# Graph attention stage of a GNN: keys computed and scattered before the queries, destination rows earlier, first loads of the edge stage in another form

## The reference

```python
Q = (x @ Wq).reshape(N, NUM_HEADS, HEAD_DIM)
K = (x @ Wk).reshape(N, NUM_HEADS, HEAD_DIM)
Q_src = Q[src]
K_tgt = K[tgt]
score = (Q_src * K_tgt).sum(axis=-1) * scale + edge_attr @ We
m = jax.ops.segment_max(score, tgt, num_segments=N)
ex = jnp.exp(score - m[tgt])
...
out = agg.reshape(N, HIDDEN) @ Wo + bo
```

## Time and profile before

| | us |
|---|---|
| median of 3 runs | 2367.73 |
| lowest and highest | 2366.19, 2367.78 |
| the profiled execution | 2364.44 |
| its span | 2362.7 |
| PE busy in the span | 1813.0 |
| DVE busy | 1230.3 |
| POOL busy | 1175.3 |
| ACT busy | 921.1 |

### The profile page before, as it was taken

One profiled execution on the slowest core, in us unless ns is written; L12 is line 12 of the kernel. 1 busy time (PEld: TensorE's weight loads), 2 busy tenths in 40 slices (PEclk: granted clock), 3 DMA queues, 4 the chain that ended last, 5 costly groups with the idle time before them and its releaser, 6 DMA issues. The chain is left out here.

```text
span 2362.7 us, 39722 instructions
## 1 busy us (share of the span) xinstructions
PE 1813.0 (77%) x12108; PEld 1537.0 (65%) x12109; DVE 1230.3 (52%) x2534; ACT 921.1 (39%) x1975; POOL 1175.3 (50%) x1175
## 2 busy tenths in 40 slices
PE   5627988887863889599950888788869449999996
PEld 4425766666653666499950776667747449999996
DVE  6527977777757521311135877777746752222221
ACT  4325765555531343344325222222224233333332
POOL 1575777777722200244425777777760014444443
PEclk9858988777776898699975999999979569999998
DMA  4397655555562110377767766666650477776775
GB/s 121 100 188 171 171 158 152 155 157 154 149 144 69 45 43 22 99 202 202 198 159 197 245 222 222 223 217 228 221 169 12 123 228 194 192 200 186 198 200 154
DMA packets 224073, 383.40 MB, mean 162 GB/s; under 512 B 38181, under 2 KB 167748, under 8 KB 223764
## 3 DMA queue, kind: packets, MB, share of 16 engines
q1 hardware_dynamic: 158988, 243.83, 33.8%
q0 software_dynamic: 64160, 136.38, 22.8%
q10 hardware_dynamic: 840, 2.16, 0.3%
HBM read 287.62 MB, written 98.35 MB: 163 GB/s over the span
## 5 line engine op out<-in xcount | busy, mean ns | idle before, releaser
L785 POOL DMA_INDIRECT qr<-q_rows,src_t x405 | 392.8, 970 | 139.4 <-issue 120.3
L1918 POOL DMA_INDIRECT fr<-f_rows,src_i x381 | 360.3, 946 | 155.5 <-issue 112.4
L1938 PE MATMUL psP<-f_part,onehot 125*128 125x256 bf16 x2925 | 358.0, 286 | 82.5 <-DVE onehot L1964 82.3
L1938 PEld LDWEIGHTS psP<-f_part,onehot 125*128 125x128 bf16 x2925 | 297.3, 103 | 136.6 <-DVE onehot L1964 90.8
L867 PE MATMUL psK<-kp,oh_k 126*128 x1680 | 286.8, 327 | 86.4 <-DVE qr L935 51.7
L867 PEld LDWEIGHTS psK<-kp,oh_k 126*128 126x128 bf16 x1680 | 189.9, 113 | 179.4 <-issue 101.7
L1976 DVE SCALAR_TENSOR_TENSOR psA<-psA,same,fr 128x256 f32<-128x256 f32 x420 | 206.4, 491 | 92.9 <-DMA fr<-f_rows,src_i 61.6
L2048 ACT ACTIVATE acc<-psA 128x1280 f32<-128x1280 f32 x84 | 103.9, 1237 | 327.3 <-DVEq L1979 320.7
L1668 ACT ACTIVATE m1hT<-m1psH,m1par 128x128 f32<-128x128 f32 x448 | 127.7, 368 | 254.0 <-PE m1psH L1688 254.0
L1688 PEld LDWEIGHTS m1psH<-m1xT,m1w 128*128 128x128 f32 x1792 | 211.0, 194 | 2.8
L1688 PE MATMUL m1psH<-m1xT,m1w 128*128 128x128 f32 x1792 | 211.2, 277 | 0.0
(11 more groups left out here) (478 smaller groups left out, 2716.6 us busy)
## 6 DMA issues: line engine op xcount, KB each, us to landing
m1w<-in_L_ffn_W_dram SPq DMA_DIRECT2D x56, 1024.0 KB, 5.9
run_rows<-acc SPq DMA_DIRECT2D x84, 640.0 KB, 3.5
m0w<-in_L_ffn_Wd_dram SPq DMA_DIRECT2D x32, 1024.0 KB, 5.5
loc<-locals_ SPq DMA_DIRECT2D x85, 157.5 KB
ea<-in_edge_attr_dram SPq DMA_DIRECT2D x84, 140.0 KB
w_all<-in_L_ffn_W_dram SPq DMA_DIRECT2D x8, 1024.0 KB
m1b<-in_L_ffn_b_dram SPq DMA_DIRECT2D x56, 128.0 KB, 2.9
qr<-q_rows,src_t POOLq DMA_INDIRECT x420
```

The lines of the kernel that those rows point to most:

```text
L785: nc.gpsimd.indirect_dma_start(out=qr[:, n % GQ, u, :], out_offset=None, in_=q_rows, in_offset=bass.IndirectOffsetOnAxis(ap=src_t[:, n, u: ...
L1918: nc.gpsimd.indirect_dma_start(out=fr[:, n % GI, u, :], out_offset=None, in_=f_rows, in_offset=bass.IndirectOffsetOnAxis(ap=src_i[:, n * G ...
L1938: last = nc.tensor.matmul(psP[:, k % 2, 0:D], onehot[:, k % 2, t, :], f_part[:, c, t, :], start=(t == 0 and c == 0), stop=(t == T - 1 and ...
```

## The change

The first stage makes the keys first and the queries last. The work on the destinations moves ahead of the statistics of groups 1 to 4. `pos_i` and the scatters no longer come after queries and gathers. ACT takes four small copies from DVE. In the edge stage, the first loads of `loc` don't wait, the keys are loaded in 5 parts (19, 15, 15, 15, 14 blocks), PE turns the edge attributes of the next group after the key expansion, and its first and last turn are written out of the loop.

```diff
-AHEAD = 3
+AHEAD = 1
...
-                store_q(0)
-                store_q(1)
                 sp.wait_ge(s_local, 2)
...
-                for i in range(2, NG):
-                    store_q(i)
+                store_q(0)
                 sp.wait_ge(s_localst, 48)
                 sp.dma_start(base_i[:], bases).then_inc(s_base, 16)
+                for i in range(1, NG):
+                    store_q(i)
...
-                pool.wait_ge(s_srck, 1)
-                pool.wait_ge(s_qst, 32 * NG)
...
-                for g in range(AHEAD - 1):
-                    gather(g)
                 pool.wait_ge(s_pos, 1)
...
-                gather(AHEAD - 1)
+                pool.wait_ge(s_srck, 1)
+                pool.wait_ge(s_qst, 32 * NG)
+                for g in range(AHEAD):
+                    gather(g)
                 pool.wait_ge(s_kst, 16 * T)
...
-                for i in range(2):
+                for i in range(NG):
                     apply_norm(i)
                     fetch_normed(i)
+                    if i == 0:
+                        first_part(0)
+                    if i == 2:
+                        first_part(1)
+                        middle_part(0)
+                        first_part(2)
+                first_part(3)
+                middle_part(1)
+                first_part(4)
                 for i in range(NG):
                     if i + 2 < NG:
-                        apply_norm(i + 2)
+                        middle_part(i + 2)
                     fetch_queries(i)
...
-            K_GROUPS = (0, 1, 2, 3)
+            K_GROUPS = (0, 1, 2, 3, 4)
...
-                load_locals(0, 0)
                 sp.wait_ge(s_eaz, 2)
                 for g in range(1, GI):
+                    load_locals(0, g - 1, reused=False)
                     load_ea(0, g, True)
                     load_k(sp, g)
-                    load_locals(0, g)
+                load_k(sp, GI)
+                load_locals(0, GI - 1)
...
+                turn_attributes(0, 0)
+                groups(0, first_turn=True)
+                with pe.Fori(1, EITER - 1) as i:
+                    groups(i)
+                groups(EITER - 1, last_turn=True)
```

More of the change, by code:

```diff
@@ L486, in key @@
                 def key(t):
+                    pe.wait_ge(s_t0, t // G + 1)
                     pe.wait_ge(s_k0e, t + 1)
@@ L506, in _, with rows @@
                 last.then_inc(s_par_turned, 1)
+                def rows(a, b):
+                    for t in range(a, b):
+                        dst_row(t)
                 turn_normed(0)
-                turn_normed(1)
[L510 to L520, removed]
@@ L521, in _ @@
-                pe.wait_ge(s_srcf, 1)
-                pe.wait_ge(s_par_kept, 1)
[L523 to L531, removed]
+                pe.wait_ge(s_w0, 32)
@@ new lines, in _ @@
+                for t in range(G):
+                    key(t)
+                pe.wait_ge(s_sel, 1)
+                pe.wait_ge(s_num, 2)
+                rows(0, 4)
+                turn_normed(1)
+                rows(4, 6)
+                key(5)
+                rows(6, 8)
+                turn_normed(2)
+                for n in range(3):
+                    key(6 + n)
+                    rows(8 + 2 * n, 10 + 2 * n)
+                key(9)
+                rows(14, 15)
+                for t in range(10, 13):
+                    key(t)
@@ L637, in _ @@
                 v.sem_inc(s_sel, 1)
[L638 to L642, removed]
+                deviations(1, 3)
+                v.wait_ge(s_const, 10)
+                ends(range(3 * G))
+                second_part(0)
+                deviations(3, NG)
+                third_part(0)
+                ends(range(3 * G, T))
+                nc.vector.scalar_tensor_tensor(end_f[:], part_n[:], float(J), end_f[:], ALU.mult, ALU.add).then_inc(s_end, 1)
+                degrees()
+                second_part(1)
+                places()
+                third_part(1)
                 v.wait_ge(s_src, 32)
                 nc.vector.tensor_copy(src_gf[:], src_g[:]).then_inc(s_srcf, 1)
+                second_part(2)
                 v.wait_ge(s_rankd, 16)
@@ L653, in _ @@
                                         ALU.subtract).then_inc(s_local, 1)
-                v.wait_ge(s_const, 10)
-                ends(range(T - 2 * G))
+                third_part(2)
+                second_part(3)
+                third_part(3)
                 v.wait_ge(s_srcT, 1)
[L657 to L668, removed]
+                nc.vector.tensor_copy(src_t[0:ET, 0:NK], psT[0:ET, 0, 0:J].rearrange("p (u k) -> p k u", u=G)).then_inc(s_srck, 1)
+                second_part(4)
+                third_part(4)
         score = sb(top, "score", [E, H, J])
@@ L844, in _ @@
                 pe.wait_ge(s_webd, 32)
-                with pe.Fori(0, EITER) as i:
-                    for g in range(GI):
[L847 to L881, removed]
-                            last = nc.tensor.matmul(psC[0:P, 0:T], oh_lo[:, g, u, :], oh_hi[:, g, u, :], start=False, stop=False,
-                                                    skip_group_check=True)
-                        last.then_inc(s_ohu, 1)
@@ new lines, in edge_scores @@
+                def edge_scores(i, g):
+                    pe.wait_ge(s_eae, i * GI + g + 1 + GI)
+                    pe.wait_ge(s_esk, i * GI + previous_use(g, 2, GI) + 1 + GI)
+                    for n in range(3):
+                        w = min(128, G * ED - n * 128)
+                        last = nc.tensor.matmul(psS[:, g % 2, n * 2 * H:n * 2 * H + w // ED * H],
+                                                eaT[0:w, g, n * E:(n + 1) * E], we2[0:w, 0:w // ED * H],
+                                                start=True, stop=True)
+                    last.then_inc(s_es, 1)
@@ new lines, in count_sources, with groups @@
+                def count_sources(i, g):
+                    pe.wait_ge(s_oh, i * GI + g + 1)
+                    for u in range(G):
+                        last = nc.tensor.matmul(psC[0:P, 0:T], oh_lo[:, g, u, :], oh_hi[:, g, u, :], start=False, stop=False,
+                                                skip_group_check=True)
+                    last.then_inc(s_ohu, 1)
+                def groups(i, first_turn=False, last_turn=False):
+                    first = named_bases(i, 0)
+                    for g in range(GI):
+                        expand(i, g, first, first_turn)
+                        if g + 1 < GI:
+                            first = named_bases(i, g + 1)
+                            turn_attributes(i, g + 1)
+                        elif not last_turn:
+                            turn_attributes(i + 1, 0)
+                        edge_scores(i, g)
+                        count_sources(i, g)
```

77 lines of the change are left out of this document (60 added, 17 removed).

## The result

| | before | after |
|---|---|---|
| median of 6 runs, us | 2367.76 | 2375.32 |
| lowest and highest | 2366.19, 2368.97 | 2373.80, 2379.24 |
| the profiled execution | 2364.44 | 2373.80 |
| first scatter, start | 87.94 | 79.03 |
| last scatter, start | 125.61 | 118.14 |

The changed kernel is slower by 7.6 us, 0.3 %: the ratio is 1.0036, with an interval of 1.0023 to 1.0049. The forecast was 2362.0, a gain. So the prediction had the wrong direction, and the time lies 6.3 us above its range.

A forecast was written before the change was run, and what follows sets the result against it. POOL's stream of gathers was taken to bound the edge stage: 123.2 + 420 x 1.274 + 1.3 = 659.6 against 665.28, 5.7 us less. Against the median 2367.73 this gave 2362.0, range 2354.5 to 2369.

The forecast's parts named there:

- What bounds the kernel: Edge stage: POOL's stream of gathers sets its end, and PE, DVE and ACT follow it.
- First scatter, 82.1: First stage: POOL's first scatter starts at 82.1 us, 5.8 earlier than 87.94.
- Last query copied, 117.0: First stage: last key leaves PE at 92.4, then 25 queries take 22 us plus 2.5 of pauses, to 117.0.
- queries at half clock: Rival, first stage: PE's clock at 0.50 makes each query 1.46 us, POOL starts at 137.9, total 2375.5; chance 0.08.
- This gives 122.0. The stores now run beside the scatters: End of first stage: query stores land 5.0 us after the last copy, plus 1.2 unhidden; first gather at 123.2.
- Ten more gathers and the stall: Edge stage: ten more gathers cost 12.7 us; the first turn's stall falls from 16.0 to 1.0 to 1.5.
- Keys in 5 parts and loads without waits, worth nothing: Edge stage's first loads: given no gain; PE may begin group 3 up to 6 us earlier, DVE still waits for `loc`.
- Pitch, 1.274 us: Edge stage: time per gather on POOL without the first turn's stall, 1.274 us, applied to 420 gathers.
- rival E: Rival from the experiments: the edge stage's edits cost 3 to 5 us at 979 ns a gather; no chance given.
- A microsecond at POOL's last gather is one of the total: After the edge stage: later stages are the same code behind the same barrier, so changes pass one to one.

The follow-up runs named there:

- e2: Changed first stage with the edge stage of the kernel before, against the kernel before: 2757.82 and 2741.52 us, ratios 1.0060 and 1.0040.
- e8: The changed kernel unaltered, run again on another chip, against the kernel before: 2762.61 us, ratio 1.0046.
- e4: Against the changed kernel, the eleventh and later scatters wait until the queries are stored: 2762.03 us.
- e7: Against the changed kernel, the eighteenth and later scatters wait until the queries are stored: 2762.11 us.
- e1: The kernel before with the edge stage of the changed one, against the kernel before: 2751.04, 2738.74, 2738.95 us, ratios 1.0005, 1.0054, 1.0028.

## Why the prediction was wrong, point by point

**What bounds the kernel: right.** In the result's executions POOL's stream of gathers still sets the end of the edge stage. Its last gather moved by +5.8 us and the profiled execution by +9.4.

**First scatter, 82.1: 3.1 us too late.** It came at 79.03. The last rows of counts and their copies ended at 69.8 instead of 72.9. The wait that I had put on key 17 is there, 3.31 us:

```profile
73.53 2.04 PE L483 MATMUL psQ<-w_qk,n_rows 128*125 128x256 f32 x4 [2.92 <-ACT k_f L443]
76.27 0.18 DVE L620 COPY tot<-psP 125x25 f32<-125x25 f32 x1 [3.31 <-PE psP L556]
```

**Last query copied, 117.0: right within 1.6.** The last key left PE at 93.2 (forecast 92.4) and the queries ran at PE's full rate:

```profile
103.50 6.74 PE L483 MATMUL psQ<-w_qk,n_rows 128*125 128x256 f32 x30 [0.18 <-ACT x L433]
```

These 30 records are 7.5 products at 0.90 us each, and the granted clock is 1.00 in the windows from 90 to 115, 2.4 GHz. So the rival "queries at half clock", which gave 2375.5, the time that came, did not happen. Only its total fits: it has the first gather at 137.9, which came at 132.14, and its mechanism is refuted. The match is luck, and it takes this row to see it.

**The step that failed: "This gives 122.0. The stores now run beside the scatters", with 1.2 us "of a bound from 0 to 3".** I had taken the 5.0 us between last copy and landing from a stretch in which nothing else was transferred, and added a bound for company. That made 6.2; measured beside scatters it is 16.7, and 17.0 to 17.6 in three more executions of this first stage (e2 twice, e8). The landing cost 10.5 us more than the sum had, of which the earlier last copy gave 1.6 back: the first gather was to be at 123.2 and came at 132.14, 8.9 us of the miss. e4 and e7 show the cause: the same stores land after 4.6 and 5.6 us when no scatter starts beside the last of them.

By the Trainium skill, "DMA: Bandwidth & Descriptors", section "Issuing engines are not separate DMA queues", transfers started by different engines interleave on the same 16 DMA engines; the trace agrees (scatters lengthen too, from 4.8 us to landing before to 7.3 in the median now). I had quoted this rule and said that it spoke for later landing, and the sum had 1.2 us for it. The rows that I did have (scatters alone at a share of 0.47) showed that half the engines' time was taken in all of the stretch; I didn't set it against the stores' own share. That was 0.46 to 0.56 in e4, so the two make 0.93 to 1.03, and a bound of 3 us on the landing had no ground.

**Ten more gathers and the stall: right.** 16.0 us of stall (an estimate from the earlier trace rows) went and the 12.8 us of ten gathers came. The waits of POOL in the edge stage are 2.4 us now.

**Keys in 5 parts and loads without waits, worth nothing: so by this trace, not shown by totals.** PE starts group 3 at 184.84, 8 us earlier than in the earlier trace rows, yet DVE waits as long as before, for `loc`:

```profile
184.84 4.14 PE L895 MATMUL psK<-kp,oh_k 126*128 x20 [4.99 <-DMA kp<-k_rows]
```

```profile
194.14 0.77 DVE L955 TENSOR_SCALAR oh_k<-loc,k_at 126x640 bf16<-126x640 bf16 x2 [13.69 <-DMA loc<-locals_]
...
197.38 1.49 DVE L991 TENSOR_REDUCE dots<-qr 128x40 f32<-128x1280 f32 x1
```

Group 3 is done at 198.87, which is 64.7 us after SP began the edge stage (134.13); before, it was 68.05 after. So the loads may have gained some 3 us, and it didn't count: POOL, which started late, never had to wait for that buffer. e1, which has these edits alone, was slower than the kernel before by 0.54 and 0.28 % on two of three chips, so a cost of them isn't excluded.

**Pitch, 1.274 us: 1.283 now,** (671.11 - 132.14) / 420, waits included, so 539.0 us where I had 536.4 with the stall: 2.6 us of the miss. The mean gather went from 970 to 979 ns. Gathers of a block that the change doesn't touch (L1067 and L1236 after, 25 in all) lengthened as well in that execution, and one kernel varied by 12 ns in the experiments. I think it chance of the execution; it isn't shown, and a part of it may be the edge stage's edits (rival E).

**"A microsecond at POOL's last gather is one of the total": not quite.** Behind the last gather the profiled executions differ by 3.5 us more, 2.3 of it in the last block, whose code is the same. By the medians (+7.6) it is 1.8. This stays open.

The miss adds up: 8.9 + 2.6 + 1.8 = 13.3 us, and 2362.0 + 13.3 = 2375.3. Only the 8.9 have a cause that experiments show; without them the time would be some 2366.4, an estimate, between the forecast and the kernel before.

## What to carry to other kernels

Before moving a transfer beside another, add up both shares of the DMA engines from windows in which each runs alone; where they came near 1 here, the last to be issued landed much later than its lone duration, and whoever waited for it waited for the backlog. A wait that "is now behind other work" is hidden only as long as that work doesn't use the same resource. When a result's total fits a rival, look for the rival's own row before believing it.

## What of the hardware was not expected

Two streams of transfers together moved less than the sum of what each moved alone, at a busy share below 1 over 5 us: 141 GB/s (0.46) and 131 (0.48) alone, 194 (0.86) together. Over 2 us, from 116 to 118, the share did reach 0.98, at 252 GB/s, so 0.86 is no ceiling. The same stores landed 4.6 us after the last copy alone and 16.7 to 17.6 beside scatters.

SP's issue of a plain store is not of fixed length: 0.40 us in the median and 1.28 at most in e4, with most stores alone, and 1.5 and 4.6 in the changed kernel beside scatters. A late landing can so begin with a late issue.

The same kernel before took 2367.8 us in the result and 2726 to 2750 on the four chips of the experiments. In 300 to 600 us of the changed kernel, PE's granted clock was 0.80 in the result and 0.69 in e8, the DMA share 0.56 and 0.41. Which comes first there, the clock or the pauses, no run tells.
